# A four-layer graph network on one core: finishing the tangential parts, the edge tables and the softmax bound at other places of the program

## The reference, cut to what matters

```
# layer 0: 4 heads, two softmaxes over the edges of each receiver
proj = einsum('nf,hfg->nhg', x, w_proj);  delta = proj[src] - proj[dst]
radial     = einsum('ehf,hf->eh', delta, radial_score) - scale * edge_weight
tangential = einsum('ehf,hf->eh', delta, tangential_score)
out = sum over both of segment_sum(softmax(logits)[:, :, None] * delta, dst)
layer0 = x + out.mean(heads) @ w_out

# layer 1: three rounds h = relu(LN(mean of h[src] @ w_l + h @ w_r)) + residual, then h @ w_fc + b_fc
# layer 2: 8 heads of 8, a bias for each edge from edge_attr_32
bias   = silu(edge_attr_32 @ We1 + be1) @ We2 + be2
scores = sum(Q[dst] * K[src]) / sqrt(8) + bias
layer2 = segment_sum(softmax(scores) * V[src], dst) @ WO + bO

# layer 3
layer3 = segment_sum(x[src] + x[dst] + edge_attr_64, dst)
```

## Time and profile before

| | us |
|---|---|
| median of three runs | 2970.07 |
| lowest, highest | 2968.24, 2970.22 |
| profiled execution, its own time | 2972.75 |
| span of its trace | 2970.9 |

### The profile page before, as it was taken

How to read it: one execution, slowest core, us unless ns; L and a number is a source line. 1 busy time by engine, 2 the same in 40 slices (tenths; PEclk the granted TensorE clock), 3 DMA queues, 4 the chain that set the end, 5 groups by cost and what they waited for, 6 DMA issues and landing times. The chain is left out here.

```text
span 2970.9 us, 64636 instructions
## 1 busy us (share of the span) xinstructions
PE 2225.6 (75%) x13922; PEld 1710.1 (58%) x13923; DVE 2083.0 (70%) x7862; ACT 631.7 (21%) x1180; POOL 1783.2 (60%) x1857
## 2 busy tenths in 40 slices
PE   0288888889888898986799557667676676676748
PEld 0255555555555555555799446656566666565637
DVE  6477777777777777747566557777777777777755
ACT  0323322333222333231000111111111111111100
POOL 0077777777777777730001167777777777777722
PEclk9999999999999999985899555555555555555558
DMA  1144554545545455542000133333333333333330
GB/s 42 55 128 133 141 142 128 142 130 145 141 129 143 126 142 141 134 88 57 20 1 2 35 77 83 81 82 82 81 81 82 81 83 81 81 82 80 82 41 12
DMA packets 425511, 268.62 MB, mean 90 GB/s; under 512 B 334070, under 2 KB 375909, under 8 KB 425445
## 3 DMA queue, kind: packets, MB, share of 16 engines
q0 software_dynamic: 71040, 176.52, 23.6%
q1 hardware_dynamic: 284418, 49.42, 8.8%
q10 hardware_dynamic: 69986, 41.88, 4.6%
HBM read 231.16 MB, written 15.97 MB: 83 GB/s over the span
## 5 line engine op out<-in xcount | busy, mean ns | idle before, releaser
L880 POOL DMA_INDIRECT edges_rows<-table,edges_idx x888 | 862.8, 972 | 290.2 <-issue 221.9
L2066 POOL DMA_INDIRECT all_arena<-table_kv,edges_idx x888 | 855.8, 964 | 276.3 <-issue 255.7
L2258 PE MATMUL edges_acc<-edges_values,edges_into 128*128 128x136 f32 x1776 | 511.4, 461 | 259.7 <-DVE edges_values L2146 237.6
L2258 PEld LDWEIGHTS edges_acc<-edges_values,edges_into 128*128 128x128 f32 x1776 | 416.6, 328 | 307.0 <-DVE edges_values L2146 286.4
L1053 PE MATMUL edges_radial_ps<-edges_rows,edges_into_w 128*128 x1776 | 461.3, 396 | 94.1 <-SPq L897 75.3
L962 DVE TENSOR_SCALAR edges_cell<-edges_ramp,edges_strip_key,first_key 128x400 bf16<-128x400 f16 x1184 | 451.2, 381 | 0.0
L1053 PEld LDWEIGHTS edges_radial_ps<-edges_rows,edges_into_w 128*128 128x128 f32 x1776 | 319.8, 190 | 219.0 <-issue 178.0
L2111 DVE TENSOR_SCALAR edges_ahead<-edges_nodes,edges_starts,edges_dst_f 128x128 bf16<-128x128 f32 x894 | 261.7, 360 | 174.3 <-issue 174.3
L961 DVE TENSOR_SCALAR edges_low<-edges_places,first_src_low 128x128 bf16<-128x128 bf16 x1184 | 332.1, 281 | 0.0
L2192 ACT COPY edges_into_t<-edges_t_ps 128x384 bf16<-128x384 bf16 x298 | 142.9, 480 | 874.0 <-PE edges_t_ps L2226 865.1
L967 DVE TENSOR_SCALAR edges_into_w<-edges_nodes,first_dst_f,first_weight 128x128 f32<-128x128 f32 x888 | 276.1, 368 | 0.0
(11 more groups left out here) (343 smaller groups left out, 2561.4 us busy)
## 6 DMA issues: line engine op xcount, KB each, us to landing
edges_values<-in_edge_attr SPq DMA_DIRECT2D x888, 32.0 KB
all_arena<-all_arena ACTq DMA_DIRECT2D x50, 400.0 KB
edges_rows<-table,edges_idx POOLq DMA_INDIRECT x888
all_arena<-table_kv,edges_idx POOLq DMA_INDIRECT x888
edges_attr<-in_edge_attr ACTq DMA_DIRECT2D x51, 256.0 KB
edges_bias<-bias_kept SPq DMA_DIRECT2D x296, 12.0 KB
bias_kept<-edges_bias_out ACTq DMA_DIRECT2D x52, 64.0 KB
table<-all_arena SPq DMA_DIRECT2D x1, 3250.0 KB, 11.4
```

The costliest lines, as they stand in the source:

```text
L880: pool.indirect_dma_start(rows[:, n, :], None, table0, bass.IndirectOffsetOnAxis(ap=idx[:, n:n + 1], axis=0)).then_inc(s_rows[g], 16)
L2066: pool.indirect_dma_start(rows[:, n, :], None, table_kv, bass.IndirectOffsetOnAxis(ap=idx[:, n:n + 1], axis=0)).then_inc(s_rows[g], 16)
L2258: last = nc.tensor.matmul(acc[:, 0:2 * F + H2], into[:, h, j, :], values[:, h, j, :], start=False, stop=True, skip_group_check=True)
```

## The change

Five edits, all outside the two edge loops' bodies.

1. Of the six roundings of `scaled` only the first stays in the set-up. The other five, the four subtractions and the clearing of `last_block` move into the `edges0` block: ScalarE does one ahead of its table preload and four after its first `load_attr`, VectorE subtracts after its index copies and memsets, and TensorE waits for all of them (`s_parts` 5) ahead of its first matmul.
2. `rows` is made and stored in two halves of 12 and 13 windows, each with a DMA of its own.
3. The four iotas move from the start of `edges0` to behind `partition_all_reduce` in the set-up's block, and the waits on `s_iota` go. Their tiles are now allocated with `src_i` and `dst_f`.
4. The edge tables for attention are loaded while the rounds run, into the free half of the big `arena`, and the ring of gathered rows starts behind them. `attend` loads them itself only in its clamped form, which is not used here.
5. The softmax bound is worked out at the end of the rounds' block. The maxima over partitions go through TensorE: a transpose of `top`, a reduce on VectorE, a diagonal matrix, and a product with ones that puts the 24 maxima on every partition. VectorE goes through the tail in an order of its own, `late`: fc 0, fc 1, fc 2, kvq 0, fc 3, kvq 1, fc 4, kvq 2, kvq 3, kvq 4. The block after the `If` goes; it is repeated inside the `If`. In sums_seen a transpose on TensorE and a reduce over one partition take the place of GpSimd's maximum.

```
@@ set-up, one block
-                        sp.wait_ge(s_rows, 1)
-                        sp.dma_start(by_node(table0), rows[:, :, :]).then_inc(s_st, 16)
-                        sp.wait_ge(s_st, 48)
+                        for n, ws in enumerate(halves):
+                            sp.wait_ge(s_rows, n + 1)
+                            sp.dma_start(by_node(table0)[:, ws, :], rows[:, ws, :]).then_inc(s_st, 16)
+                        sp.wait_ge(s_st, 64)
...
                         pool.partition_all_reduce(top_all[:, :, :].rearrange("p a n -> p (a n)"),
                                                   top[:, :, :].rearrange("p a n -> p (a n)"), P, RMAX).then_inc(s_all, 1)
+                        pool.iota(places[:, :], [[1, P]], base=0, channel_multiplier=0, allow_small_or_imprecise_dtypes=True)
+                        pool.iota(ramp[:, :], [[1, KEY]], base=0, channel_multiplier=0, allow_small_or_imprecise_dtypes=True)
+                        pool.iota(strip_key[:, :], [[KEY, Q]], base=-Q * KEY, channel_multiplier=0,
+                                  allow_small_or_imprecise_dtypes=True)
+                        pool.iota(nodes[:, :], [[1, P]], base=-P, channel_multiplier=0, allow_small_or_imprecise_dtypes=True)
...
-                        for k in range(H0):
-                            c0 = k // 2 * PAIR + k % 2 * F
-                            step(dve.tensor_tensor(rows[:, :, c0:c0 + F], x_in[:, :, :], over(factor_r[:, :, k], F), ALU.mult))
-                        step(dve.tensor_copy(rows[:, :, 2 * F:PAIR], factor_r[:, :, 0:2]))
-                        dve.tensor_copy(rows[:, :, PAIR + 2 * F:ROW0], factor_r[:, :, 2:4]).then_inc(s_rows, 1)
+                        for ws in halves:
+                            for k in range(H0):
+                                c0 = k // 2 * PAIR + k % 2 * F
+                                step(dve.tensor_tensor(rows[:, ws, c0:c0 + F], x_in[:, ws, :], over(factor_r[:, ws, k], F), ALU.mult))
+                            step(dve.tensor_copy(rows[:, ws, 2 * F:PAIR], factor_r[:, ws, 0:2]))
+                            dve.tensor_copy(rows[:, ws, PAIR + 2 * F:ROW0], factor_r[:, ws, 2:4]).then_inc(s_rows, 1)
...
-                        for n in range(2):
-                            for k in range(2):
-                                dve.wait_ge(s_cast, 2 * n + k + 1)
-                                dve.tensor_tensor(scaled[:, k, :, :], scaled[:, k, :, :], head_part(k, n), ALU.subtract).then_inc(s_part, 1)
-                        dve.memset(last_block[:, :, :], 0.0).then_inc(s_part, 1)
...
-                        for n in range(3):
-                            for k in range(2):
-                                act.wait_ge(s_part, 2 * n + k + 1)
-                                act.copy(head_part(k, n), scaled[:, k, :, :]).then_inc(s_cast, 1)
+                        act.wait_ge(s_part, 1)
+                        act.copy(head_part(0, 0), scaled[:, 0, :, :]).then_inc(s_cast, 1)
@@ edges0: VectorE, TensorE, ScalarE
-                        dve.wait_ge(s_zero, 9)
-                        dve.wait_ge(s_iota, 4)
+                        dve.memset(last_block[:, :, :], 0.0).then_inc(s_zero, 1)
+                        for n in range(2):
+                            for k in range(2):
+                                if n or k:
+                                    dve.wait_ge(s_parts, 2 * n + k)
+                                dve.tensor_tensor(scaled[:, k, :, :], scaled[:, k, :, :], head_part(k, n), ALU.subtract).then_inc(s_less, 1)
+                        dve.wait_ge(s_zero, 10)
...
-                        pe.wait_ge(s_zero, 9)
-                        pe.wait_ge(s_iota, 4)
+                        pe.wait_ge(s_zero, 10)
                         pe.wait_ge(s_w, 16 * 12)
+                        pe.wait_ge(s_parts, 5)
...
+                        act.copy(head_part(1, 0), scaled[:, 1, :, :]).then_inc(s_parts, 1)
                         act.preload_act_table(ACT.Silu)
...
                         load_attr(slice(0, BATCH))
-                        act.wait_ge(s_zero, 9)
+                        for n in (1, 2):
+                            for k in range(2):
+                                act.wait_ge(s_less, 2 * n + k - 1)
+                                act.copy(head_part(k, n), scaled[:, k, :, :]).then_inc(s_parts, 1)
+                        act.wait_ge(s_zero, 10)
@@ rounds: tables on SP, VectorE's order, the bound in the block
+                late = [("fc", 0), ("fc", 1)]
+                for i in range(2, GR):
+                    late += [("fc", i), ("kvq", i - 2)]
+                late += [("kvq", GR - 2), ("kvq", GR - 1)]
...
+                        sp.dma_start(edge_src, src_kept).then_inc(s_x, 16)
+                        sp.dma_start(edge_dst, dst_kept).then_inc(s_x, 16)
...
+                        root_on_gpsimd(pool, 1)
...
+                        pe.wait_ge(s_top, 1)
+                        nc.tensor.transpose(turned_ps[0:3 * H2, 0, :], top[:, :], ident[:, :]).then_inc(s_top_t, 1)
+                        pe.wait_ge(s_spread, 1)
+                        nc.tensor.matmul(out_ps[:, 1, 0:3 * H2], ones[:, :], top_t[:, 2:2 + 3 * H2], start=True, stop=True).then_inc(s_all, 1)
...
+                                if g == GR - 1:
+                                    tops(dve, 1)
                                 split_group(step, dve, group4(q3, g), tmp[:, :, :], kvq[:, g % 2, :, 0:F]).then_inc(s_split, 1)
                                 dve.wait_ge(s_split, g + 1)
+                        dve.wait_ge(s_top_t, 1)
+                        step(dve.tensor_reduce(top_t[:, 0:1], turned_ps[0:3 * H2, 0, :], AX, ALU.max))
+                        step(dve.tensor_scalar(top_t[:, 1:2], top_t[:, 0:1], 1e37, None, ALU.min))
+                        dve.tensor_scalar(top_t[:, 2:2 + 3 * H2], ident[0:3 * H2, 0:3 * H2], top_t[:, 1:2], None, ALU.mult).then_inc(s_spread, 1)
+                        dve.wait_ge(s_all, 1)
+                        step(dve.tensor_copy(top_all[:, :], out_ps[:, 1, 0:3 * H2]))
+                        bound_on_vector(step, dve, 1)
@@ attend
-                            sp.dma_start(src_i[:, :], src_kept).then_inc(s_ld, 16)
-                            sp.dma_start(dst_f[:, :], dst_kept).then_inc(s_ld, 16)
+                            if clamped:
+                                sp.dma_start(src_i, src_kept).then_inc(s_ld, 16)
+                                sp.dma_start(dst_f, dst_kept).then_inc(s_ld, 16)
...
-                            dve.wait_ge(s_ld, 32)
+                            if clamped:
+                                dve.wait_ge(s_ld, 32)
@@ sums_seen
-                    @block.gpsimd
-                    def _(pool):
-                        pool.wait_ge(s_low, 1)
-                        pool.partition_all_reduce(low[:, 1:2], low[:, 0:1], P, RMAX).then_inc(s_all, 1)
+                    @block.tensor
+                    def _(pe):
+                        pe.wait_ge(s_low, 1)
+                        nc.tensor.transpose(low_ps[0:1, :], low[:, 0:1], ident[:, :]).then_inc(s_all, 1)
...
-                        step(dve.tensor_scalar(low[:, 2:3], low[:, 1:2], 0.0, None, ALU.is_gt))
-                        step(dve.tensor_copy(flags[:, 2:3], low[:, 2:3]))
+                        step(dve.tensor_reduce(low[0:1, 1:2], low_ps[0:1, :], AX, ALU.max))
+                        step(dve.tensor_scalar(low[0:1, 2:3], low[0:1, 1:2], 0.0, None, ALU.is_gt))
+                        step(dve.tensor_copy(flags[0:1, 2:3], low[0:1, 2:3]))
```

103 lines of the change are left out of this document (58 added, 45 removed).

## The result

The changed kernel takes **2939.14 us** (median of 4 runs, 2935.42 to 2946.23) where the kernel before takes 2970.07 (median of 3 runs; a fourth, at 7149.23 us, was disturbed and is left out here and in the ratio). That is 30.9 us less; the ratio is 0.9898 with a 95% interval of 0.9886 to 0.9909. The forecast was 2940.0, in a range of 2932 to 2949, from a sum of 29.8 us.

What follows compares the result with a forecast made beforehand. Two edge loops, paced by GpSimd's gathers, hold 2291 of 2971 us; the change starts them earlier. Terms 10.0 + 0 + 11.6 + 3.7 + 4.5 = 29.8 us off 2970.07 give 2940.3, stated as 2940, range 2932 to 2949.

Steps and rivals of the forecast that it cites:

- The set-up's block: Set-up's last block: with the table stored in halves it ends at 119.0 in place of 134.69, 15.7 us earlier.
- The parts in the first layer's block: Entry to the first layer: subtractions 122.9 to 137.0, last rounding 137.1 to 140.1, six gathers over by 129.
- The start of the loop: First edge loop: the whole loop moves 10.0 us earlier, between ends of 7.2 and 12.
- The order `late`: Tail of the rounds: VectorE's new order gains 0, since the tail hangs on TensorE and ScalarE alternating.
- The bound: Softmax bound moved into the rounds' block: attention starts 11.6 us earlier, ends 10 and 12.5.
- The tables: Attention's entry: tables loaded during the rounds bring the first index copy 3.7 us earlier, ends 2.5 and 4.2.
- sums_seen: Maximum through TensorE in sums_seen: 1.2 us from reduce to flag in place of 5.7, 4.5 gained.
- one of its signs: Attention: its loop starting near 1695.1, which is 1720.4 less 10.0, 11.6 and 3.7, would show the forecast right.
- rival A: First loop hardly moves, 5 us in place of 10, and softmax bound 10; 2946.5 us, 17%.
- Rival C: Second loop's gathers slow down with the ring further on in `arena`; 2984 us, 3%.
- D: Whole kernel: no measurable gain, since stages regain the waits elsewhere; 2968 us, 2%.
- B: More won: sequencer ahead of the subtraction, GpSimd's 12 us carried on, seams a microsecond cheaper each; 2935 us, 15%.

Runs made afterwards that it cites:

- e5: The changed kernel with the first layer's table stored in one transfer instead of two halves; 2938.01 us in one run.
- e1: The changed kernel run again with no edit; 2938.02 us, ratio 0.9891.
- e6: The changed kernel with the softmax bound's maxima by GpSimd's reduce over partitions, in the changed place, instead of through TensorE; 2941.36 us, ratio 0.9908.
- e9: The changed kernel with VectorE's last groups of the rounds in the old order instead of `late`; 2936.98 us in one run.
- e10: The changed kernel with the tables of indices and targets loaded at attention's entry, not in the rounds; 2948.2 us in one run.
- e3: The changed kernel with the four iotas back in the first layer's block, ahead of the gathers; 2938.98 us, ratio 0.9896.
- e7: The changed kernel with TensorE waiting for the parts where it first reads them, not ahead of its loop; 2938.50 us, ratio 0.9899.
- e2: The kernel before with only the four iotas moved to the set-up's last block; 2964.34 us over 10 runs, ratio 0.9979.
- e12: The kernel before plus a GpSimd reduce over partitions of an unread scratch tile behind attention's last gather; 2964.81 us over 10 runs, ratio 0.9986.

## Why the prediction came out right, point by point

**1. The set-up's block** ended at 118.8; forecast 119.0. The DMA view of after has the halves, of 13 and 12 windows; the whole table took 11.4 us, before and in e5:

```profile
table<-all_arena SPq DMA_DIRECT2D x1, 1690.0 KB, 7.0
table<-all_arena SPq DMA_DIRECT2D x1, 1560.0 KB, 6.2
```

If all three moved at one rate, 1.8 us of each are not transfer (7.0 + 6.2 less 11.4), near the 2 assumed. The first half, of 12 windows, landed 6.2 us after 107.1, at 113.3; the second, issued near 111.7, landed near 118.7, against forecasts of 113.5 and 118.5 to 119. VectorE, at 118.8, came last by a hair. The sentence in which a fixed part paid a second time behind the first half would end the block at 121 did not come true: the second half was issued 1.7 us before the first had landed. e5 shows what the halves are worth: 4 us at the entry.

**2. The parts in the first layer's block**: subtractions from 122.7, forecast 122.9; the last rounding from 136.67 to 139.61, forecast 137.1 to 140.1. What was wrong there is "1.22 us each, over by 129": the sixth gather was over at 138.7, because beside VectorE's subtractions a gather takes 3.2 to 3.6 us. It cost nothing, since VectorE's L958 came later still, at 139.06.

**3. The start of the loop.** L958 at 139.06, forecast 140.1 in the early case. The term was 10.0 and the last gather moved by 9.9 (8.4 in e1). The heads moved by 9.9 in e1, where the drain is 1.5 us shorter than before. That the two numbers agree to 0.1 us is luck: e6, e9 and e10 have the same first layer, and there the last gather moved by 10.9, 9.6 and 5.5. The size was right within that scatter, and a part of its reasoning was not: that GpSimd "was what came last, and part of its lead counts". In e3 1.8 us of the lead went at no cost, and in the changed kernel VectorE's third L958 (147.36) waited 2.54 us for TensorE, of which e7 takes 2.4 off. Of the 11.4 us at the entry, and 12.2 at the 7th gather, 10.8 were left at the 72nd and 9.7 at the 432nd. That the parts and the ramps had to be moved together is something the prediction did not separate: the ramps alone give 6.2 (e2), and put back cost nothing (e3).

**4. The order `late`**: 0 forecast, 0.2 measured (e9).

**5. The bound**: VectorE's last step ended at 1679.83, 8.66 us behind the start of kvq 4, where it was 3.64, so 5.0 later as forecast; the barriers took 6.1, forecast 5.3 and 0.8. Attention's iota came 11.6 us earlier against kvq 4 than the stage's first load did before. Forecast 11.6. With GpSimd doing the maxima in the new place (e6) it would have been 8.0, and not zero, as the prediction read the rule: most of the term is the place. The Trainium skill (GPSIMD Engine Reference, 4.1 Engine selection) gives such maxima to GpSimd; the trace doesn't agree, by those 3.6 us.

**6. The tables**: index copy 1.45 us behind the stage's start, forecast 1.5; 3.7 against 3.7 (e10: 4.1 to 4.4 when undone).

**7. sums_seen**: 4.55 against 4.5. As e12 shows, TensorE is not needed for this: with the switch paid early GpSimd's reduce gives 4.8.

**The sum** of what was measured is 9.9 + 0.2 + 11.6 + 3.7 + 4.55, 30.0 us, against 29.8. The spans differ by 37.2: 6.3 more in the drain, and about 1.0 in places that no step named (0.2 in heads and rounds, 0.2 in the second loop, 0.2 at the `If` behind it, 0.3 in `last`). What the prediction lacked was any word of the drain: it took off the 2.7 us by which the profiled execution of before lay over the median, but did not look at the clock at the loop's end, by which two profiles of one kernel can lie 6 us apart. So one of its signs came out wrong in the first profile and right in the second: attention's loop was to start near 1695.1 and started at 1688.5, and at 1694.9 in e1. First L958, at 139.06 and 139.87, lay just under its 140 to 143.5. Two of its sums are off and change nothing: rival A's terms give 23.2, not 23.5, and the upper ends give 2936, from which two microseconds of scatter reach 2934, not 2932. Rival A (5 us at the loop, 10 at the bound) is excluded by the 11.6 at the bound and by 8.4 to 10.9 at the loop in four profiles of this first layer; in the fifth, e10, the gain was still 9.8 at the 432nd gather and fell to 5.5 behind it. Rival C is excluded by 1125.0 against 1125.3 us for the same 888 gathers with the ring further on (1120.8 to 1126.7 in all profiles, far from 44 us more), and D by all. Of B, the sequencer running ahead is true, and the rest is not.
